# First attention: the projection's bias as three bf16 rows of a TensorE product, four buffers of input rows

## The reference

```
x = x + L0_xattn(layernorm(x), ctx, ctx)      # 16 heads of 16 values, q and k normalised per head
    # inside: ... o = softmax(q k^T) v ; return o @ Wp.T + bp
x = x + L0_moe(layernorm(x))                  # 8 experts, top 2
x = x + L1_xattn(layernorm(x), ctx, ctx)
x = x + L1_ffn(layernorm(x))                  # 32 experts, top 4, and a shared expert
```

## Time and profile before

| | |
|---|---|
| median of 3 runs | 1449.73 us (1448.69 to 1450.63) |
| span of the profiled execution, first to last instruction | 1446.9 us |
| the profiled execution's own time | not given by the page |
| mean granted TensorE clock, share of full speed | 0.953 |
| busy over the span: PE / DVE / ACT / POOL | 91% / 54% / 41% / 45% |
| first attention, from its first copy to its last router result | 110 to 371 us |

### The profile page before, as it was taken

One profiled execution on the slowest core, in us unless ns is written; L12 is line 12 of the kernel. 1 busy time (PEld: TensorE's weight loads), 2 busy tenths in 40 slices (PEclk: granted clock), 3 DMA queues, 4 the chain that ended last, 5 costly groups with the idle time before them and its releaser, 6 DMA issues. The chain is left out here.

```text
span 1446.9 us, 29194 instructions
## 1 busy us (share of the span) xinstructions
PE 1322.9 (91%) x7743; PEld 1053.3 (73%) x7744; DVE 777.4 (54%) x2053; ACT 589.1 (41%) x1314; POOL 648.1 (45%) x873
## 2 busy tenths in 40 slices
PE   7988999999879999999999499947999999989994
PEld 4666777777558888888888377714888888848883
DVE  4874888887742222222222588784233333337774
ACT  2454777777322222222222266625433333322110
POOL 1213565665113333333332255403655555257775
PEclk9998999999799999999999699956999999999998
DMA  2107322222731111111111665353555555845554
GB/s 95 59 30 307 114 89 90 80 93 99 289 120 44 51 51 51 51 51 51 51 51 36 207 194 175 117 236 120 185 161 162 163 162 152 131 124 160 161 165 131
DMA packets 108684, 175.75 MB, mean 121 GB/s; under 512 B 16698, under 2 KB 83275, under 8 KB 105292
## 3 DMA queue, kind: packets, MB, share of 16 engines
q1 hardware_dynamic: 72276, 96.09, 19.5%
q0 software_dynamic: 20736, 56.65, 14.7%
q10 hardware_dynamic: 15608, 22.25, 4.3%
HBM read 115.13 MB, written 59.77 MB: 121 GB/s over the span
## 5 line engine op out<-in xcount | busy, mean ns | idle before, releaser
L1228 POOL DMA_INDIRECT xg<-t_xn,token x160 | 151.4, 946 | 154.7 <-PE psum L2088 69.3
L2162 POOL DMA_INDIRECT su_yg<-t_y,slot x128 | 124.2, 970 | 68.4 <-issue 37.5
L2100 PE MATMUL psum<-gu,m_xT 128*128 x640 | 153.3, 383 | 0.0
L1403 DVE TENSOR_TENSOR m_h<-psum,m_h 128x512 f32<-128x512 f32 x72 | 49.7, 690 | 163.7 <-ACT m_h L1378 163.7
L1465 PE MATMUL psum<-w,m_hT 128*128 x576 | 136.4, 380 | 0.8 <-ACT m_hT L1384 0.8
L2100 PEld LDWEIGHTS psum<-gu,m_xT 128*128 128x128 f32 x640 | 116.5, 192 | 13.0 <-issue 0.2
L1444 PE MATMUL psum<-w,m_xT_high 128*128 x288 | 120.5, 419 | 0.0
L2059 DVE TENSOR_TENSOR m_h<-psum,m_sg 128x256 f32<-128x256 f32 x80 | 33.9, 424 | 159.0 <-ACT m_sg L2038 159.0
L1444 PE MATMUL psum<-w,m_xT_low 128*128 x288 | 114.4, 397 | 0.0
L1444 PE MATMUL psum<-w_low,m_xT_high 128*128 x288 | 113.7, 395 | 0.0
L1465 PEld LDWEIGHTS psum<-w,m_hT 128*128 128x128 f32 x576 | 103.8, 190 | 12.4 <-issue 1.2
(11 more groups left out here) (305 smaller groups left out, 3119.8 us busy)
## 6 DMA issues: line engine op xcount, KB each, us to landing
t_y<-m_y SPq DMA_DIRECT2D x80, 256.0 KB, 2.2
w<-in_w SPq DMA_DIRECT2D x8, 1024.0 KB, 11.4
t_x<-at_x SPq DMA_DIRECT2D x64, 128.0 KB, 1.9
t_w_low<-at_low ACTq DMA_DIRECT2D x64, 128.0 KB, 1.7
w_low<-t_w_low SPq DMA_DIRECT2D x8, 1024.0 KB, 13.3
at_yg<-t_y SPq DMA_DIRECT2D x32, 256.0 KB, 2.8
gu<-in_gu ACTq DMA_DIRECT2D x8, 1024.0 KB, 12.4
w<-in_x SPq DMA_DIRECT2D x16, 256.0 KB, 2.7
```

The lines of the kernel that those rows point to most:

```text
L1228: pool.indirect_dma_start(out=g.xg1[j % GB][:, k * D:(k + 1) * D], out_offset=None, in_=g.xn4, in_offset=bass.IndirectOffsetOnAxis(ap=g.to ...
L2100: last = pe.matmul(ps_gu[p][:, k * 2 * M1:(k + 1) * 2 * M1], xT[p][:, at:at + P], g.gu[:, bass.ds(ex[k] * (DC * 2 * M1) + c * 2 * M1, 2 * ...
L2162: pool.indirect_dma_start(out=yg[p][k][:, :], out_offset=None, in_=g.y1, in_offset=bass.IndirectOffsetOnAxis(ap=g.slot[:, at:at + 1], axis ...
```

## The change

The bias is no longer added by POOL. At the start of the phase, bp is loaded as 16 x 16 values, DVE splits it in three bf16 pieces whose sum is exactly the float32 value (three casts, two subtractions), and SP moves the pieces to three partitions (`bias3`, 3 x 256). For each tile, TensorE begins the accumulation of `ps_wp` with a product of 3 rows of ones (`ones3`) and `bias3`. DVE then adds `x_in` itself to `ps_wp`. `x_in` has four buffers in place of two, `xb` and its semaphore are gone; the load of tile t waits until x1 of tile t - 4 is done. SP's unrolled steps are 8 with a body of 4, before 6 with a body of 2.

```diff
-        bp = sb("bp", [P, D])
+        bp, left = sb("bp", [H, DH]), sb("left", [H, DH])
+        pieces = [sb(f"piece{i}", [H, DH], BF16) for i in range(3)]
+        bias3, ones3 = sb("bias3", [3, D], BF16), sb("ones3", [3, P], BF16)
...
-        x_in = [sb(f"x_in{i}", [P, D]) for i in range(2)]
-        xb = [sb(f"xb{i}", [P, D]) for i in range(2)]
+        x_in = [sb(f"x_in{i}", [P, D]) for i in range(4)]
...
         def _(sp):
-            for dst, src in ((wp, g.ins["wp"]), (wr, g.ins["wr0"]), (bp, g.ins["bp"])):
+            sp.dma_start(bp[:, :], g.ins["bp"].rearrange("o (h d) -> (o h) d", d=DH)).then_inc(s_bp, 16)
+            for dst, src in ((wp, g.ins["wp"]), (wr, g.ins["wr0"])):
                 sp.dma_start(dst[:, :], src).then_inc(s_w, 16)
...
             def input_rows(t):
-                wait(sp, xb_ready, t.shift(-1).n)
-                sp.dma_start(x_in[t.mod(2)][:, :], g.ins["x"][bass.ds(t.n * P, P), :]).then_inc(s_x[t.mod(2)], 16)
+                wait(sp, x1_done, t.shift(-3).n)
+                sp.dma_start(x_in[t.mod(4)][:, :], g.ins["x"][bass.ds(t.n * P, P), :]).then_inc(s_x[t.mod(4)], 16)
...
             for t in range(2):
                 input_rows(At(None, 0, t))
+            for i in range(3):
+                sp.wait_ge(s_piece, i + 1)
+                sp.dma_start(bias3[i:i + 1, :], pieces[i][:, :]).then_inc(s_b3, 16)
             for e in range(1, E0 - W13_LATE):
                 expert_weights(e)
...
-            steps(sp, 6, NT, NT + 4, 2, tile)
+            steps(sp, 8, NT, NT + 4, 4, tile)
...
         def _(pool):
-                t = tile_at(u, 4 + LEAD)
-                if t is not None:
-                    p = t.mod(2)
-                    if t.loop is None and t.off == 0:
-                        pool.wait_ge(s_w, 3 * 16)
-                    pool.wait_ge(s_x[p], (t.div(2).n + 1) * 16)
-
-                    wait(pool, x1_done, t.shift(-1).n)
-                    pool.tensor_tensor(xb[p][:, :], x_in[p][:, :], bp[:, :], ALU.add).then_inc(xb_ready, 1)
...
         def _(dve):
             dve.memset(ps_raw, 0.0).then_inc(ps_clear, 1)
+            dve.memset(ones3[:, :], 1.0).then_inc(s_one3, 1)
+            dve.wait_ge(s_bp, 16)
+            for i in range(3):
+                rest = left if i else bp
+                if i:
+                    dve.wait_ge(s_left, i)
+                dve.tensor_copy(pieces[i][:, :], rest[:, :]).then_inc(s_piece, 1)
+                if i < 2:
+                    dve.wait_ge(s_piece, i + 1)
+                    dve.tensor_tensor(left[:, :], rest[:, :], pieces[i][:, :], ALU.subtract).then_inc(s_left, 1)
...
-                    dve.wait_ge(xb_ready, t.n + 1)
+                    dve.wait_ge(s_x[t.mod(4)], (t.div(4).n + 1) * 16)
 
                     wait(dve, x1_st[p], t.div(2).n * 16)
-                    dve.tensor_tensor(x1[p][:, :], ps_wp, xb[p][:, :], ALU.add).then_inc(x1_done, 1)
+                    dve.tensor_tensor(x1[p][:, :], ps_wp, x_in[t.mod(4)][:, :], ALU.add).then_inc(x1_done, 1)
...
                     if t.loop is None and t.off == 0:
-                        pe.wait_ge(s_w, 3 * 16)
+                        pe.wait_ge(s_w, 2 * 16)
+                        pe.wait_ge(s_one3, 1)
+                        pe.wait_ge(s_b3, 3 * 16)
                     pe.wait_ge(o_out, t.n + 1)
                     wait(pe, x1_done, t.n)
+                    pe.matmul(ps_wp, ones3[:, :], bias3[:, :], start=True, stop=False)
                     for c in range(DC):
                         last = pe.matmul(ps_wp, oT[p][:, c * P:(c + 1) * P], wp[:, c * D:(c + 1) * D],
-                                         start=(c == 0), stop=(c == DC - 1))
+                                         start=False, stop=(c == DC - 1))
```

More of the change, by code:

```diff
@@ L502, in attention0_phase @@
         wr = sb("wr", [P, DC * E0])
-        bp = sb("bp", [P, D])
+        bp, left = sb("bp", [H, DH]), sb("left", [H, DH])
+        pieces = [sb(f"piece{i}", [H, DH], BF16) for i in range(3)]
+        bias3, ones3 = sb("bias3", [3, D], BF16), sb("ones3", [3, P], BF16)
+        s_bp, s_piece, s_left, s_b3, s_one3 = (sem(n) for n in ("s_bp", "s_piece", "s_left", "s_b3", "s_one3"))
         q_s = [sb(f"q_s{i}", [P, D]) for i in range(2)]
@@ L525, in attention0_phase @@
             "s_w", "s_next", "s_w13_first", "s_w13", "w_high", "w_low", "w_round"))
-        s_x, x1_st, xn_st = ([sem(f"{n}{i}") for i in range(2)] for n in ("s_x", "x1_st", "xn_st"))
+        s_x = [sem(f"s_x{i}") for i in range(4)]
+        x1_st, xn_st = ([sem(f"{n}{i}") for i in range(2)] for n in ("x1_st", "xn_st"))
         low_st = [sem(f"low_st{i}") for i in range(4)]
         v_ready = sem("v_ready")
-        k_ready, q_ready, xb_ready, s_mm, mx_ready, sub_done, exp_done, tp_mm, tp_out, pv_mm, rec_ready, o_norm = (
-            sem(n) for n in ("k_ready", "q_ready", "xb_ready", "s_mm", "mx_ready", "sub_done", "exp_done", "tp_mm",
+        k_ready, q_ready, s_mm, mx_ready, sub_done, exp_done, tp_mm, tp_out, pv_mm, rec_ready, o_norm = (
+            sem(n) for n in ("k_ready", "q_ready", "s_mm", "mx_ready", "sub_done", "exp_done", "tp_mm",
                              "tp_out", "pv_mm", "rec_ready", "o_norm"))
@@ L2334 @@
         "wp": cols(a["L0_xattn_Wp"]),
-        "bp": row(a["L0_xattn_bp"]),
+        "bp": a["L0_xattn_bp"][None, :],
         "gb": np.stack([np.tile(a["L0_xattn_" + n], HG) for n in ("q_gamma", "q_beta", "k_gamma", "k_beta")], 1),
```

## The result

The changed kernel takes 1455.8 us (median of 15 runs, 1451.9 to 1461.9); the kernel before, run beside it, 1450.2 us (15 runs, 1447.7 to 1454.9). The ratio is 1.0041 with a 95% interval of 1.0031 to 1.0051, which is 5.9 us, 4.5 to 7.4: slower by more than 0.2%. I had forecast 1455.4.

The account below looks back on a forecast made before the run. The prediction took PE's stream to bound the steady stretch: +6.1 us for the bias product, -0.4 for POOL's relief, 0 at the start, +5.7 in all on 1449.7, giving 1455.4 us. The range ran from 0.8 us below 1452.6 to 1459.2 us.

Parts of the forecast that it names:

- PE sets the pace: Steady stretch, 140 to 350 us: PE is always busy, so time added to its stream lengthens the phase one for one.
- The product at 0.21 us, 29 times, +6.1: Bias product ahead of the projection, costed from the same operation in the phase before: 0.21 us for 29 tiles, +6.1 us.
- The lower end, 0.13: Bias product's low cost per tile, one L445 record, if shape changes cost no more than today's one: +3.8 us.
- The upper one, 0.31: Bias product's high cost per tile, if the 0.10 us handing over is paid in front as well: +9.0 us.
- the step from L805: PE's step into the bias product, taken as equally dear as today's 0.57 us step to L833, shape change included.
- B: Rival: the bias product pays a change of shape on both sides, +9.5 us in all, 1459.2 us; 12 in 100.
- POOL's addition, -0.4: Removing L649 from POOL: 0 in the steady stretch; in the drain half of a possible -0.9 us, so -0.4 us.
- L483 at 0.15 in the drain: Expected sign in the later profile: DVE's copy L483 takes 0.15 us in the drain, not 0.59 beside POOL's L640.
- The start, 0: Start of the phase: DVE's bias split and SP's small loads are covered, 0 us; ends 0 and +0.5.
- A: Rival: the bias product costs its stream alone, 29 x 0.13, with full drain relief: +2.9 us, 1452.6 us; 12 in 100.
- C: Rival: the bias product is covered by waits on PE and nothing changes there: 1449.3 us; 7 in 100.
- D: Rival: DVE sets the steady period and POOL's addition slows it, so the change is faster: -7.8 us, 1441.9 us; 3 in 100.

## Why the prediction was right

**PE sets the pace: right, and shown.** The period follows PE's stream in every kernel (7.478 without the product, 7.500, 7.689, 7.798), and no product of PE waits for an engine, except with the product behind the projection.

**The product at 0.21 us, 29 times, +6.1: right.** 28 x 0.21 = 5.88 in the table, and once more in the 29th tile. The lower end, 0.13, is near what a product costs whose rows match those of its neighbour (0.12), but by luck: it was the length of a float32 record of 128 columns. The upper one, 0.31, is what the change of shape costs on both sides, and the product behind the projection pays it and 0.05 more. That the step from L805 would be no dearer held (0.56 against 0.57), so B falls. What I had left open is where the 0.21 comes from: 0.12 of stream and 0.09 of a changed height.

**POOL's addition, -0.4: right in kind, right in size by luck.** Against the one profile of before, the relief is 0.68 us with the product and 0.69 without it, but only 0.44 of it goes when POOL has its addition back. I had expected 0.44 for each of two L483 and took half. Both came free, and each shortens the step behind it by only 0.24 and 0.30, the drain by 0.44 in all. The sign "L483 at 0.15 in the drain" was too broad: another one, beside three L647 that run from 373.23 to 375.37, is still held, as at 368.15 before:

```profile
374.80 0.59 DVE L483 COPY top_v<-at_top 128x8 f32<-128x8 f32 x1
```

The other 0.24 us of the 0.68 is not shown to be the addition's. In the drain of before, one L108 on POOL starts 0.52 us after the end of the L137 that it waits for; the same one starts after 0.20 in each of the other eleven profiles, also with the addition back. Before, then with the addition back:

```profile
360.83 0.18 DVE L137 BATCH_NORM_AGGREGATE at_ln_mv<-at_ln_stats 128x2 f32<-128x6 f32 x1 [0.16 <-DVE at_ln_stats L132]
361.53 0.22 POOL L108 TENSOR_SCALAR at_ln_rstd<-at_ln_mv 128x1 f32<-128x1 f32 x1 [2.36 <-DVE at_ln_mv L137]
```

```profile
366.72 0.18 DVE L137 BATCH_NORM_AGGREGATE at_ln_mv<-at_ln_stats 128x2 f32<-128x6 f32 x1 [0.16 <-DVE at_ln_stats L132]
367.10 0.22 POOL L108 TENSOR_SCALAR at_ln_rstd<-at_ln_mv 128x1 f32<-128x1 f32 x1 [2.05 <-DVE at_ln_mv L137]
```

With one profile of before, whether this lies in the kernel or in that execution stays open. In the steady stretch nothing comes of the missing addition, though POOL now waits 0.90 us a tile longer, where 0.7 was forecast: the period's 0.21 goes to POOL's slack as well.

**The start, 0: right.** In the changed kernel the scores start at 113.37 and DVE's first reduction at 115.83, 2.46 us later, as in the kernel before (112.04 and 114.50). So the split of the bias is hidden, with 0.42 us to spare:

```profile
112.10 2.39 POOL L637 TENSOR_TENSOR at_kblk<-kv,hmask 128x616 f32<-128x616 f32 x2
...
113.38 1.14 DVE L666 TENSOR_TENSOR at_left<-at_bp,at_piece 16x16 f32<-16x16 f32 x1
...
115.24 0.16 DVE L663 CAST at_piece<-at_left 16x16 bf16<-16x16 f32 x1
115.83 0.80 DVE L673 TENSOR_REDUCE at_mx<-psum 128x8 f32<-128x616 f32 x1 [0.42 <-PE psum L785]
```

A subtraction was held by POOL's L637 (1.14 us), and DVE still waited 0.42 us for PE. I had named a cast as what would be held, and the time 114.5 for L673, which came at 115.83 because the phase before, whose code is the same, ended 1.33 us later in this execution.

**The sum.** Forecast +5.7. By the parts of the phase, 29 x 0.21 = +6.1, less 0.68, +5.4, or +5.6 with 0.44 alone; by the ratio +5.9, 4.5 to 7.4. All lie within the interval.

**The other rivals.** A (the stream alone, +2.9) fell on the shape, and holds for the kernel with 96 or 128 rows, which does better than A: net 0.02 a tile. C fell, since nothing on PE was waiting. D fell in the steady stretch.

Once the change costs nothing, it gives nothing either: with 128 rows the two timings are 0.9992 and 1.0001, both with 1 in their interval, and so has the addition two half steps earlier. No version here beats the kernel before by a measurable time. What stays open is the spread behind the phase, 1073.8 to 1081.5 us, whose cause I did not look for.

## What to carry to other kernels

Moving work from an engine with slack to the one that sets the pace costs what it adds to that engine's stream, once per tile, however small it is: look up which engine has waits in the steady stretch, and multiply the gap between starts of the very operation (not its recorded duration) by the tiles. A product of few rows ahead of a full-height one is worth padding with zeros to its height: here it fell from 0.21 to 0.02 us a tile, and with it the whole loss. Between two full-height ones only the 3-row form was measured, at 0.36. Judge a change of a few us by the parts of the phase that it touches, since two profiles of one kernel differed by 2.9 us in span.

## What the runs showed of the hardware

- The step from a product of 3 or 32 rows to one of 128 costs 0.09 us (0.21 against 0.12), and the step from 128 down to 3 costs 0.10 (1.06 against 0.96), at the full clock. With 96 or 128 rows ahead of 128 there is none: the next product's weights load under it, and the load that was exposed behind the 77-row product is covered too (0.96 to 0.87 us).
- A DVE copy of 0.17 us beside a queue of POOL instructions doesn't wait for one of them but, every fourth tile with the product behind the projection, for several (1.80 us, L643 and two L647 in the instance shown).
